# Folding weights and keys of a cross attention ahead of it, and packing its folded values in 12 transfers

## What is computed

```python
x = x + _L0_attn_ref(_layernorm(x, axis=-1), ...)     # 16 heads of 8, causal
x = x + _L0_xattn_ref(_layernorm(x, axis=-1), ctx_768, mask, g_norm, null_kv, Wq, Wkv, Wout, g_out)
```

## Time and profile before

| | us |
|---|---|
| median of 3 runs | 1479.56 |
| lowest, highest | 1476.8, 1482.32 |
| profiled execution | 1480.19 |
| its span | 1478.1 |

### The profile page before, as it was taken

How to read it: one execution, slowest core, us unless ns; L and a number is a source line. 1 busy time by engine, 2 the same in 40 slices (tenths; PEclk the granted TensorE clock), 3 DMA queues, 4 the chain that set the end, 5 groups by cost and what they waited for, 6 DMA issues and landing times. The chain is left out here.

```text
span 1478.1 us, 29446 instructions
## 1 busy us (share of the span) xinstructions
PE 1353.3 (92%) x11618; PEld 878.8 (59%) x11618; DVE 943.0 (64%) x1906; ACT 666.9 (45%) x1690; POOL 345.6 (23%) x373
## 2 busy tenths in 40 slices
PE   8998879999999988998898987889998999999986
PEld 6776547444766666557786766774444556654434
DVE  6776365442466745455667357678888976677755
ACT  4885432442377735343511243514556777740002
POOL 4001122000111110003304011047776646400001
PEclk9998789999899999999899999999999999999998
DMA  3000011400000000000030302010111111499980
GB/s 131 2 3 2 12 26 74 143 28 28 16 2 2 2 17 1 10 12 4 2 140 26 103 12 84 3 43 29 43 29 39 21 23 23 107 215 247 250 208 15
DMA packets 27356, 80.60 MB, mean 55 GB/s; under 512 B 5375, under 2 KB 9934, under 8 KB 26838
## 3 DMA queue, kind: packets, MB, share of 16 engines
q1 hardware_dynamic: 26358, 75.60, 19.0%
q10 hardware_dynamic: 864, 3.15, 0.8%
HBM read 72.17 MB, written 1.08 MB: 50 GB/s over the span
## 5 line engine op out<-in xcount | busy, mean ns | idle before, releaser
L194 PE MATMUL psum<-ident 128*128 128x128 f32 x1324 | 172.0, 289 | 13.2 <-DVE var L144 5.9
L194 PEld LDWEIGHTS psum<-ident 128*128 128x128 f32 x1324 | 163.2, 202 | 21.2 <-DVE var L144 6.8
L185 POOL TENSOR_TENSOR rstd<-var,minus_half 128x4 f32<-128x4 f32 x30 | 30.6, 1022 | 564.6 <-DVE var L144 527.4
L568 DVE TENSOR_REDUCE quad_max<-psum 128x1 f32<-128x128 f32 (+3 forms) x256 | 113.2, 484 | 57.4 <-PE psum L430 55.3
L525 ACT ACTIVATE pt<-psum,quad_max 128x128 f32<-128x128 f32 (+3 forms) x256 | 133.3, 530 | 25.8 <-DVE quad_max L568 25.7
L2862 PE MATMUL psum<-pt,slots 128*128 128x512 f32 x256 | 114.7, 599 | 5.9 <-DVE pt L3015 5.2
L2841 PE MATMUL psum<-slots,xn_t 128*128 128x512 f32 x256 | 111.0, 592 | 3.1 <-DVEq L2986 3.1
L2600 ACT ACTIVATE p<-psum,duo_max 128x512 f32<-128x512 f32 x128 | 86.7, 683 | 42.3 <-DVE duo_max L2635 42.1
L2862 PEld LDWEIGHTS psum<-pt,slots 128*128 128x128 f32 x256 | 47.1, 189 | 72.6 <-issue 48.6
L2930 ACT ACTIVATE pt<-psum,p 128x64 f32<-128x64 f32 x256 | 57.9, 392 | 69.6 <-POOL wide L3072 43.7
L2635 DVE TENSOR_REDUCE duo_max<-psum 128x1 f32<-128x512 f32 x128 | 82.2, 685 | 9.3 <-PE psum L2511 4.3
(11 more groups left out here) (511 smaller groups left out, 2822.8 us busy)
## 6 DMA issues: line engine op xcount, KB each, us to landing
pt<-scratch_out_gates SPq DMA_DIRECT2D x32, 256.0 KB, 13.6
heads<-scratch_out_gates SPq DMA_DIRECT2D x24, 256.0 KB, 16.8
slots<-in_s_l0f SPq DMA_DIRECT2D x8, 514.0 KB, 3.3
wide<-scratch_gates SPq DMA_DIRECT2D x8, 512.0 KB, 8.0
slots<-in_s_l3v SPq DMA_DIRECT2D x8, 512.0 KB, 3.6
context_v<-scratch_out_gates SPq DMA_DIRECT2D x16, 256.0 KB, 18.2
slots<-in_s_l3o ACTq DMA_DIRECT2D x6, 512.0 KB, 10.5
weights<-in_w_l1a SPq DMA_DIRECT2D x1, 2624.0 KB, 9.4
```

Of the source, the lines that this page charges most:

```text
L194: nc.tensor.matmul(m.ps[bank][:, 0:P], m.ident[:, :], m.ident[:, :], start=True, stop=True, skip_group_check=True)
L568: nc.vector.tensor_reduce(m.quad_max[:, n % 2, g:g + 1], m.ps[g][:, 0:keys], AX.X, ALU.max, negate=True).then_inc(m.quad_negmax, 1)
```

## The change

- Folded weights: made by TensorE in the last step of the self attention, ahead of the last set's value products (`fold_weights`, called by beside_last), in banks 0 to 3; ScalarE copies them out after the self attention's output.
- Keys: projected behind the self attention's share product and ahead of its output projection (`project_keys`), in banks 0 to 2, three, three and two pairs in one bank; three copies instead of eight.
- Folded keys: made behind the output projection (`fold_keys`), in banks 4 and 5, 0 and 1, 2 and 4; six copies as before. Two semaphores count all of it (folded, fold_taken).
- The bias of the output projection is added to x in the middle of the self attention, at set 16, on VectorE (`add_bias`).
- Folded values lie in another order (head, then batch and half), and so do the packed ones (chunk, then batch and half); a piece takes both batches and both halves, 4 x 128 numbers or 2 KB a partition on both sides. SyncE issues 12 transfers, all behind the copy of the last two folded values.
- Semaphores pair_zero and sig_aug_ready are gone; their waits go to turned_zero (one count more in the last stage) and sig_g_ready (count 3).

The core of the diff (left out: the renamed semaphores):

```diff
@@ -449,7 +449,7 @@
-def quad_tensor(nc, pe, m, a, q, k, values, q_ready, v_ready, project, ramp):
+def quad_tensor(nc, pe, m, a, q, k, values, q_ready, v_ready, project, ramp, beside_last=None):
     def share(group):
@@ -477,6 +477,8 @@
...
             quad_turn(nc, pe, m, a, n, 1)
+        if i == SETS + 1 and beside_last:
+            beside_last()
         n = i - 2
@@ -627,7 +629,8 @@
...
                 values=lambda g, b, j, kt: m.head_vals[:, j, b * NQ + kt, own(g)],
-                q_ready=q_ready, v_ready=v_ready, project=None, ramp=ramp)
+                q_ready=q_ready, v_ready=v_ready, project=None, ramp=ramp, beside_last=lambda: fold_weights(nc, pe, m))
+    project_keys(nc, pe, m)
     pe.wait_ge(m.quad_scaled, B)
@@ -723,11 +726,12 @@
+    def add_bias(dve):
+        m.dve.done(nc.vector.tensor_tensor(m.x[:, :, :], m.x[:, :, :],
+                                           w["bo"].rearrange("p (o d) -> p o d", o=1).broadcast_to([P, NT, P]), ALU.add))
     quad_vector(nc, dve, m, a, lambda b: nc.vector.reciprocal(m.quad_share[:, b, :, :], m.quad_sum[:, b, :, :]),
-                before={j: lambda dve, j=j: head_queries(j) for j in range(1, 4)})
-    m.dve.done(nc.vector.tensor_tensor(m.x[:, :, :], m.x[:, :, :],
-                                       w["bo"].rearrange("p (o d) -> p o d", o=1).broadcast_to([P, NT, P]), ALU.add))
+                before={j: lambda dve, j=j: head_queries(j) for j in range(1, 4)} | {SETS // 2: add_bias})
     add_to_x(nc, dve, m, "l0y", twice=True)
@@ -898,43 +902,67 @@
+FOLD_BANKS = ((4, 5), (0, 1), (2, 4))
+FOLDS = H // 4 + len(KEY_PAIRS) + 2 * len(KEY_PAIRS)
+def fold_weights(nc, pe, m):
+    w = m.w["l0x"]
+    pe.wait_ge(m.loaded["l0x"], 16)
+    for n in range(2):
+        for i in range(4):
+            g = 4 * n + i
+            for e in range(2):
+                rows = slice(64 * e, 64 * e + 64)
+                last = nc.tensor.matmul(m.ps[2 * n + e][0:DC + 1, i * P:(i + 1) * P],
+                                        w["wv"][rows, g * (DC + 1):(g + 1) * (DC + 1)], w["wo"][rows, g * P:(g + 1) * P],
+                                        start=True, stop=True)
+                if i == 3:
+                    last.then_inc(m.folded, 1)
+def project_keys(nc, pe, m):
+    w = m.w["l0x"]
+    pe.wait_ge(m.context_in, 16 * 4)
+    for n, pairs in enumerate(KEY_PAIRS):
+        pe.wait_ge(m.fold_taken, n + 1)
+        for i, g in enumerate(pairs):
+            last = nc.tensor.matmul(m.ps[n][:, i * B * SC:(i + 1) * B * SC], w["wk"][0:DC, g * P:(g + 1) * P],
+                                    m.context_t[0:DC, :], start=True, stop=True)
+        last.then_inc(m.folded, 1)
+def fold_keys(nc, pe, m):
+    w, nk = m.w["l0x"], L0X.nk
+    pe.wait_ge(m.keys_zero, 2)
+    for n, pairs in enumerate(KEY_PAIRS):
+        banks = FOLD_BANKS[n]
+        pe.wait_ge(m.fold_taken, H // 4 + len(KEY_PAIRS) + (1 if n == 2 else 0))
+        for i, g in enumerate(pairs):
+            for e in range(2):
+                rows = slice(64 * e, 64 * e + 64)
+                last = nc.tensor.matmul(m.ps[banks[e]][:, i * B * nk:(i + 1) * B * nk], w["wq"][rows, g * P:(g + 1) * P],
+                                        m.keys_own[rows, :, g * nk:(g + 1) * nk], start=True, stop=True)
+                if g == pairs[-1]:
+                    last.then_inc(m.folded, 1)
 def l0_cross_tensor(nc, pe, m):
...
     a.s0, a.x0 = m.steps0["l0x"], m.cross0["l0x"]
-    pe.wait_ge(m.loaded["l0x"], 16)
-    pe.wait_ge(m.context_in, 16 * 4)
-    for g in range(NPAIR):
-        bank = fill(m, pe, f"l0xk{g}")
-        nc.tensor.matmul(bank[:, 0:B * SC], w["wk"][0:DC, g * P:(g + 1) * P], m.context_t[0:DC, :], start=True,
-                         stop=True).then_inc(filled(m, f"l0xk{g}"), 1)
-    pe.wait_ge(m.keys_zero, 2)
-    for n, pairs in enumerate(KEY_PAIRS):
-        banks = [fill(m, pe, f"l0xa{2 * n + e}") for e in range(2)]
-        for i, g in enumerate(pairs):
-            copied(m, pe, f"l0xk{g}")
-            for e in range(2):
-                rows = slice(64 * e, 64 * e + 64)
-                last = nc.tensor.matmul(banks[e][:, i * B * nk:(i + 1) * B * nk], w["wq"][rows, g * P:(g + 1) * P],
-                                        m.keys_own[rows, :, g * nk:(g + 1) * nk], start=True, stop=True)
-                if g == pairs[-1]:
-                    last.then_inc(filled(m, f"l0xa{2 * n + e}"), 1)
-    for n in range(2):
-        banks = [fill(m, pe, f"l0xg{2 * n + e}") for e in range(2)]
-        for i in range(4):
-            g = 4 * n + i
-            for e in range(2):
-                rows = slice(64 * e, 64 * e + 64)
-                last = nc.tensor.matmul(banks[e][0:DC + 1, i * P:(i + 1) * P], w["wv"][rows, g * (DC + 1):(g + 1) * (DC + 1)],
-                                        w["wo"][rows, g * P:(g + 1) * P], start=True, stop=True)
-                if i == 3:
-                    last.then_inc(filled(m, f"l0xg{2 * n + e}"), 1)
+    fold_keys(nc, pe, m)
     busy_through_norm(nc, pe, m, 2, 0, 0)
...
     turned(nc, m, pe, "l0xn")
-    for n in range(2 * len(KEY_PAIRS)):
-        copied(m, pe, f"l0xa{n}")
+    pe.wait_ge(m.fold_taken, FOLDS)
     pe.wait_ge(m.low_row_ready, 1)
@@ -952,9 +980,6 @@
...
             bank = fill(m, pe, f"l0xb{n}")
-            if n == 0:
-                for i in range(H // 4):
-                    copied(m, pe, f"l0xg{i}")
             nc.tensor.matmul(bank[0:nk, :], m.context_null[0:DC + 1, b * nk:(b + 1) * nk],
@@ -963,12 +988,12 @@
...
             if b == 0:
-                pe.wait_ge(m.packed_in, 16 * B * len(PIECES))
+                pe.wait_ge(m.packed_in, 16 * len(PIECES))
             fill(m, pe, name)
...
             rows = chunk_rows(c)
-            last = nc.tensor.matmul(bank, m.packed[0:rows, b, half, c, :], m.xpt[0:rows, half, c, :], start=half == 0 and c == 0,
+            last = nc.tensor.matmul(bank, m.packed[0:rows, c, 2 * b + half, :], m.xpt[0:rows, half, c, :], start=half == 0 and c == 0,
                                     stop=half == 1 and c == CHUNKS - 1)
@@ -985,13 +1010,12 @@
-    for b in range(B):
-        for n in range(2):
-            copied(m, sp, f"l0xb{4 * b + 2 + n}")
-        for h, lo, hi in PIECES:
-            first = lo - h * (SC + 1)
-            sp.dma_start(m.packed[lo % P:lo % P + hi - lo, b, :, lo // P, :],
-                         m.folded_values[first:first + hi - lo, 2 * b:2 * b + 2, h * P:(h + 1) * P]).then_inc(m.packed_in, 16)
+    for n in range(B * H // 4 - 2, B * H // 4):
+        copied(m, sp, f"l0xb{n}")
+    for h, lo, hi in PIECES:
+        first = lo - h * (SC + 1)
+        sp.dma_start(m.packed[lo % P:lo % P + hi - lo, lo // P, :, :],
+                     m.folded_values[first:first + hi - lo, h, :, :]).then_inc(m.packed_in, 16)
@@ -999,23 +1023,31 @@
...
     act.wait_ge(m.keys_zero, 1)
-    for g in range(NPAIR):
-        bank = read(m, act, f"l0xk{g}")
-        nc.scalar.activation(m.keys_own[:, :, g * nk:g * nk + SC], bank[:, 0:B * SC].rearrange("p (b k) -> p b k", k=SC),
-                             ACT.Copy).then_inc(emptied(m, f"l0xk{g}"), 1)
+    taken = 0
+    def folded(bank):
+        act.wait_ge(m.folded, taken + 1)
+        return m.ps[bank]
+    for n in range(H // 4):
+        half, e = divmod(n, 2)
+        to = m.folded_weights[0:DC + 1, 8 * half:8 * half + 8, :].rearrange("p (g e) d -> p e g d", e=2)
+        nc.scalar.activation(to[:, e], folded(n)[0:DC + 1, :].rearrange("p (g d) -> p g d", d=P),
+                             ACT.Copy).then_inc(m.fold_taken, 1)
+        taken += 1
+    for n, pairs in enumerate(KEY_PAIRS):
+        count = len(pairs)
+        to = m.keys_own[:, :, pairs[0] * nk:(pairs[-1] + 1) * nk].rearrange("p b (g k) -> p g b k", k=nk)[:, :, :, 0:SC]
+        nc.scalar.activation(to, folded(n)[:, 0:count * B * SC].rearrange("p (g b k) -> p g b k", b=B, k=SC),
+                             ACT.Copy).then_inc(m.fold_taken, 1)
+        taken += 1
     for n, pairs in enumerate(KEY_PAIRS):
         for e in range(2):
-            bank = read(m, act, f"l0xa{2 * n + e}")
             count = len(pairs)
             to = m.folded_keys[:, :, 2 * pairs[0]:2 * pairs[-1] + 2, :].rearrange("p b (g e) k -> p e g b k", e=2)
-            nc.scalar.activation(to[:, e], bank[:, 0:count * B * nk].rearrange("p (g b k) -> p g b k", b=B, k=nk), ACT.Copy,
-                                 scale=64 ** -0.5).then_inc(emptied(m, f"l0xa{2 * n + e}"), 1)
-    for n in range(H // 4):
-        half, e = divmod(n, 2)
-        bank = read(m, act, f"l0xg{n}")
-        to = m.folded_weights[0:DC + 1, 8 * half:8 * half + 8, :].rearrange("p (g e) d -> p e g d", e=2)
-        nc.scalar.activation(to[:, e], bank[0:DC + 1, :].rearrange("p (g d) -> p g d", d=P),
-                             ACT.Copy).then_inc(emptied(m, f"l0xg{n}"), 1)
+            nc.scalar.activation(to[:, e], folded(FOLD_BANKS[n][e])[:, 0:count * B * nk].rearrange(
```

(18 more changed lines are left out.)

8 lines of the change are left out of this document (4 added, 4 removed).

## The result

The changed kernel takes 1461.82 us (median of 4 runs, 1456.04 to 1462.8), the kernel before beside it 1480.94 (4 runs, 1476.8 to 1485.42): a ratio of 0.9862, 95% interval 0.9823 to 0.9902. Forecast were 1460.5 and a range of 1454 to 1468. The same program timed again (experiment 3) took 1460.77 (4 runs) against 1479.96, ratio 0.9877, 0.9849 to 0.9904. The profiled execution is the quickest of the first four: 1456.04, span 1454.2.

A forecast was written before the change was run, and what follows sets the result against it. TensorE, busy 92% of the span, was taken to bound the kernel where it idles or runs at half clock. Prologue 15.6 plus packing 3.8 gave 19.4 us off 1480.19: 1460.8, as a median about 1460.5 us, range 1454 to 1468.

The forecast's parts named there:

- the prologue: Folded weights and keys moved before the cross attention's first score product, which comes earlier: 15.6 us gained, ends 8.0 and 16.5.
- the packing: 12 transfers instead of 24 ahead of the first value product: TensorE waits 5.1 us, not 8.9, 3.8 us gained.
- the bias add: Bias add of x moved on VectorE in front of set 16's maxima: 0.3 us lost, bound 0 to 1.2.
- the key projections: In the gap before the output projection: 16 records take about 3.0 us at full clock, their issue not halving.
- the folded weights inside the last step: 32 records in the self attention's last step take 3.3 us; GpSimd's scaling of o_t comes 2.0 us later.
- the issue: SyncE's issue of each packing transfer: 0.70 us, 8.4 us for 12, ends 7.1 and 10.6.
- Landing: From the last packing issue until the packed values are in: 2.8 us, between estimates of 2.2 and 3.1.
- Clock at half throughout: Rival: short TensorE gaps hold the prologue's clock at 0.50; gain 11.8 us, 1468 us; chance 0.15.
- Cheap transfers and no fall: Rival: packing issues of 0.59 us, fast rows, clock holding in the wait; gain 23.6 us, 1456 us; chance 0.14.
- Rows in pieces: Rival: packed rows stay in 512 B pieces, about 1.4 us an issue; gain 11.0 us, 1469 us; chance 0.06.
- Slower: Rival: packing behind the last folded value eats the gain, deciding from 2.3 us per transfer, 1490 us at 3.2; chance 0.03.
- No change: Rival: self-attention delay from bias add and weights meets the prologue's gain; in all under 7.4 us; chance 0.04.

The follow-up runs named there:

- experiment 3: The changed kernel timed again as it is, on another chip: 1460.77 us against 1479.96 for the kernel before, ratio 0.9877.
- experiments 1 and 3: First: the changed kernel with the 24 packing transfers of before, 1461.56 us. Second: the changed kernel again as it is, 1460.77 us.
- experiment 9: The changed kernel with the bias add of x back behind the self attention on VectorE: one execution, 1463.39 us.
- experiment 4: The changed kernel with 12 transfers in the old layout, four runs of 512 B per partition instead of one of 2 KB: one execution, 1463.27 us.
- experiment 5: The changed kernel with the 34-row packing transfer issued first, not eleventh: one execution, 1463.9 us.
- experiments 6 and 7: The changed kernel with old layout and 24 transfers, each batch's value products waiting for its own 12: 1444.44 us; the same again, 1447.81 us.
- experiments 7 and 11: First: waits split by batch, timed again, 1447.81 us. Second: that kernel with folded weights behind the last shares and output projection before key projections, 1451.64 us.
- experiment 8: The changed kernel with a bank fill and 16 unused products on TensorE ahead of the packing wait: one execution, 1463.99 us.

## Why the prediction was right, and where it was not

**The total** was right: 19.4 us were forecast, and the medians give 19.1 (1480.94 - 1461.82) and 19.2 (1479.96 - 1460.77). Two errors of opposite sign, 1.5 us too little for the prologue and 1.0 to 2.2 too much for the packing, cancel in it; that it is so close is luck. (Two slips of the sum do not matter: 139.4 and 1.5 give 140.9, not 140.7, and 1479.56 - 19.4 is 1460.2, not 1460.5.)

**The prologue, 15.6 forecast, 17.1 measured** (17.3 in A, with the clock fallen as before, experiments 1 and 3, less 0.2 for the bias add ahead of it). The mechanism was as written; two terms were dear, the key projections and VectorE's distance:
- the folded weights inside the last step, 3.3 us: 1.99 with the clock up, 2.62 to 3.73 with it down. The shares were to end 8.2 us behind the GpSimd copy (140.7 - 132.53) and end after 8.13 in experiment 3, 6.6 with the clock up;
- the key projections, 3.0 us: 2.2 from their start to the output projection's. The 16 records take less than half of the 5.4 us of before: from record to record it is 0.13 us and was 0.26, so the claim that their issue does not halve was wrong, and the row of 4.69 us held short waits for ScalarE to empty one bank after the other;
- so the output projection, which was to start 11.6 us behind the copy (144.1 - 132.53), starts after 10.66, nearly all of it from the key projections, and VectorE's add 1.10 behind it where I had 1.55, from eight records of another line;
- key folding, 2.7 us: 2.51; the norm at its old distance, the last tokens to the first score 1.5: both as predicted;
- the bias add, a loss of 0.3 (bound 1.2): 0.19 where it stands, and a gain of 0.7 where it stood (experiment 9), which no term held. The place on the timeline of before that could have said it was GpSimd's product of 2.17 us beside VectorE's add of 1.22, which I read as the product's own duration.

**The packing, 3.8 forecast, 1.6 to 2.8 measured** (B of the first profile, and of the packing alone; the ratio of the packing alone holds no change). The wait was placed right: TensorE reaches it 6.1 us behind the first issue, as worked out. The term that was mis-sized is the issue: 0.70 us each was forecast from the mean of two kinds of rows, and it is 0.81 (9.67 us for 12). The long run per partition, by which I went from 0.88 towards 0.59, saves only 0.07 to 0.09 an issue (10.76 to 9.67 us for 12 in experiment 4, 0.2 of it one long issue); the row of 0.59 was a transfer of another kind, 16 rows of 4 KB. Landing was forecast as 2.8 and is 2.5, of which the 34-row transfer makes 0.5 (experiment 5). So the wait is 6.05 us, not 5.1, where no issue is disturbed; 6.6 and 7.3 where one issue took 1.25 and 2.03 us. Against the wait of before the undisturbed packing gains 2.8 us. The clock fell in it and the slow steps behind it stayed, as written.

**The rivals.** *Clock at half throughout:* the clock was 1.00 in the output projection and the key folding in both profiles; only the folded weights and the records beside them ran at half clock, in some executions. *Cheap transfers and no fall:* neither came. *Rows in pieces:* even where they do (experiment 4) it costs 1 us, not 8, so its price of 1.4 us an issue was wrong as well. *Slower:* no issue came near 2.3 us but one of 2.03. *No change:* the self attention's delay was about 0.2 us.

What I did not ask is what the first value product waits for. All four packed quarters stood behind one wait, before and after, though the first half of them concern batch 0 alone, and 12 of the 24 transfers were early. The change keeps that wait and starts the first transfer 7.6 us later against the scores; the price of it, 8.6 us with undisturbed issues and 8.9 and 10.5 in the two profiles of the changed kernel, is more than everything that 12 transfers in place of 24 could bring (experiments 6 and 7).

**Open.** Why a single issue took 2.03 and 1.25 us in the two profiles of the changed kernel and 1.52 and 1.58 in experiments 7 and 11, when no issue of these transfers in the other profiles was over 1.06. Why the clock falls at 134 us in one execution and not in the next: in the 13 profiles it held in the four where GpSimd's copy came at 131.05 to 132.12 us and fell in the nine where it came at 132.38 to 133.25, but what links the two no run shows. Why the unchanged code behind the stage takes 1224.1 to 1237.0 us from profile to profile; a part is clock: 10 us of one later stage in the kernel before, busy time by engine and granted clock:

```profile
718.00:728.00 10.00, 9.94 (x124) 7.35 (x117) 4.54 (x7) 4.08 (x5) 3.38 (x3) 0.50 0.01 2
```

And 10 us of the same stage in the changed kernel:

```profile
695.00:705.00 10.00, 7.78 (x176) 6.00 (x171) 8.05 (x13) 5.54 (x8) 4.81 (x4) 1.00 0.01 2
```

That stage takes 79.8 us there and 72.6 here. Such swings are why 1 us gained in place can't be seen in the medians.

## What to carry to other kernels

Before transfers are merged to make them cheaper, look at which of them the waiting instruction needs: a wait split by what it uses was worth 8.6 to 10.5 us here, and half the transfers with rows four times as long 3 at best. Work that does not depend on the result at hand belongs into the gap in front of that result, where it costs only its own length and keeps the clock up; here it gave 17 us. Compare local distances between two fixed instructions, with the clock beside them, when the rest of the program moves by more than the gain that you look for.

## What the runs showed of the hardware

- The length of a SyncE issue hardly followed the bytes or the number of runs: the median is 0.83 us for two runs of 512 B a partition and for four, and 0.76 for one of 2 KB, each time over transfers of 6 to 78 rows. The shortest of the packing alone, 0.62 us, is that of 34 rows, ahead of that of 6 rows with 0.69.
- GpSimd's product of two SBUF tensors, 128x512, took 1.27 us alone and 2.17 beside a VectorE add of two SBUF tensors. The Trainium skill ("GPSIMD Engine Reference", "1. Specifications") says that GpSimd shares its SBUF interfaces with VectorE and contends with its instructions that have two SBUF inputs; the trace agrees, and shows the size: 0.9 us longer for an overlap of 1.05 us with the add.
- After 16 products ahead of a wait of 2.44 us, the clock held through the wait and fell 1 us after work had begun again (experiment 8); in the wait of 6.56 us of experiment 3 it was 0.53 over the last 2.7 us.
